# Products of the identity with itself on TensorE, in the openings and the router's end of a two-layer decoder

## The reference

```
x = x + attn0(ln(x)); x = x + xattn0(ctx, ctx, ln(x)); x = x + depths(ln(x))
x = x + attn1(ln(x)); x = x + xattn1(ln(x), ctx, ctx, mask); x = x + experts(ln(x))
```

## Time and profile before

| | |
|---|---|
| median of three runs | 2678.63 us (2676.26 to 2680.16) |
| profiled execution, its own time | 2679.13 us |
| its span | 2677.0 us |
| TensorE busy | 2317.4 us (87%) |
| VectorE, ScalarE, GpSimd busy | 1441.4, 1135.1, 738.9 us |
| mean granted clock of TensorE | 0.927 |

### The profile page before, as it was taken

One profiled execution on the slowest core, in us unless ns is written; L12 is line 12 of the kernel. 1 busy time (PEld: TensorE's weight loads), 2 busy tenths in 40 slices (PEclk: granted clock), 3 DMA queues, 4 the chain that ended last, 5 costly groups with the idle time before them and its releaser, 6 DMA issues. The chain is left out here.

```text
span 2677.0 us, 44222 instructions
## 1 busy us (share of the span) xinstructions
PE 2317.4 (87%) x13938; PEld 1441.6 (54%) x13939; DVE 1441.4 (54%) x3865; ACT 1135.1 (42%) x2659; POOL 738.9 (28%) x852
## 2 busy tenths in 40 slices
PE   4999999779984587679999999878888689999998
PEld 2455555445552344323444343344556489999997
DVE  3676666337764324267777777444554833343333
ACT  1666566423331324237777777522222023333332
POOL 3111111143322202323223222043331323333333
PEclk8999999889996799869999999978997799999999
DMA  4232222100001440022222222000005512222221
GB/s 149 73 96 92 77 85 85 37 3 5 5 1 57 66 71 1 18 84 72 67 66 72 72 65 71 23 27 9 9 5 210 183 32 34 36 37 35 35 34 25
DMA packets 134894, 148.75 MB, mean 56 GB/s; under 512 B 25374, under 2 KB 119240, under 8 KB 134600
## 3 DMA queue, kind: packets, MB, share of 16 engines
q1 hardware_dynamic: 121048, 128.83, 16.2%
q0 software_dynamic: 13680, 17.84, 4.1%
HBM read 100.71 MB, written 46.01 MB: 55 GB/s over the span
## 5 line engine op out<-in xcount | busy, mean ns | idle before, releaser
L447 ACT ACTIVATE self_probs<-self_score_ps 128x512 f32<-128x512 f32 (+3 forms) x1024 | 481.5, 516 | 331.9 <-PE self_score_ps L768 169.2
L586 DVE TENSOR_REDUCE self_neg_max<-self_max_ps 128x1 f32<-128x512 f32 x512 | 329.3, 686 | 157.3 <-PE self_max_ps L754 151.5
L754 PE MATMUL self_max_ps<-self_k_stack,self_q_stack 96*128 96x512 bf16 (+3 forms) x1024 | 355.4, 351 | 38.1 <-DVE self_neg_max L583 17.4
L765 PE MATMUL self_score_ps<-self_q_stack,self_k_stack 99*128 99x512 bf16 (+3 forms) x1024 | 345.1, 345 | 1.6 <-ACT self_probs L447 1.6
L2171 ACT ACTIVATE x_stream<-experts_up_ps,experts_bias_now 128x128 f32<-128x128 f32 x568 | 162.5, 369 | 373.2 <-PE experts_up_ps L2392 373.2
L583 DVE CUSTOM_DVE_ANT_0 self_masked<-self_max_ps,self_later 128x128 f32<-128x128 f32 (+3 forms) x512 | 235.3, 488 | 119.1 <-PE self_max_ps L754 107.7
L2392 PEld LDWEIGHTS experts_up_ps<-experts_tileT,x_stream 128*128 128x128 f32 x2272 | 266.7, 193 | 5.1 <-issue 1.6
L2392 PE MATMUL experts_up_ps<-experts_tileT,x_stream 128*128 128x128 f32 x2272 | 267.2, 276 | 1.2 <-DVE x_stream L2308 1.2
L2402 PE MATMUL experts_down_ps<-experts_down,x_stream 128*128 x1136 | 256.8, 379 | 0.0
L779 PE MATMUL self_out_ps<-self_probs,self_values 128*32 128x512 f32 (+3 forms) x2048 | 232.1, 525 | 3.3 <-ACT self_probs L447 1.4
L2402 PEld LDWEIGHTS experts_down_ps<-experts_down,x_stream 128*128 128x128 f32 x1136 | 210.4, 190 | 25.7
(11 more groups left out here) (281 smaller groups left out, 3804.8 us busy)
## 6 DMA issues: line engine op xcount, KB each, us to landing
self_parts_dram<-self_parts SPq DMA_DIRECT2D x64, 384.0 KB, 2.4
self_q_stack<-self_parts_dram SPq DMA_DIRECT2D x384, 64.0 KB, 2.3
self_k_stack<-self_parts_dram SPq DMA_DIRECT2D x384, 64.0 KB, 2.3
experts_up<-moe_up_dram SPq DMA_DIRECT2D x8, 1024.0 KB, 8.3
experts_down<-moe_down_dram SPq DMA_DIRECT2D x8, 1024.0 KB, 10.6
x_stream<-x_dram SPq DMA_DIRECT2D x8, 512.0 KB, 8.4
expert_rows_dram<-experts_down SPq DMA_DIRECT2D x8, 512.0 KB, 6.1
out_dram<-x_stream SPq DMA_DIRECT2D x8, 512.0 KB, 8.1
```

The lines of the kernel that those rows point to most:

```text
L447: act.activation(probs[:, i % 8, 0:w], score_ps[:, (16 * n + i) % 3, 0:w], ACT.Exp).then_inc(exp_done, 1)
L586: dve.tensor_reduce(neg_max[:, n % 2, t, h:h + 1], max_ps[:, i % 2, 0:w], AX, ALU.max, negate=True).then_inc(max_read, 1)
L754: last = pe.matmul(max_ps[:, i % 2, 0:w], q_stack[0:ROWS, h, P * t:P * t + P], k_stack[0:ROWS, h, 0:w], start=True, stop=True)
L765: last = pe.matmul(score_ps[:, m % 3, 0:w], k_stack[0:KROWS, head, P * j:P * j + P], q_stack[0:KROWS, head, S - w:S], start=True, stop=not ...
```

## The change

A helper, `spin`, issues a number of products of the identity with itself into a PSUM bank that nobody reads at that point. No semaphore is touched. It is called

- in both self-attentions: 24 products before TensorE's first waits; 4 before each sum of squares of the opening (with norms only); 12 (without norms) or 16 (with) behind the opening's part up to the maxima's turn; one behind each of the 32 first maximum tiles; 4 between the first sixteen and the turn of the maxima,
- in both cross-attentions: 20 before the first transposes, 4 before the first maxima, 6 before the third, 8 before the transposes of batch 2,
- in the routed one also 8, 8, 16 and 16 before the last two batches' `sr` and `bk`,
- in the depths stage: 60 before `attend(0)`.

```diff
@@ -52,6 +52,12 @@
         eng.sem_inc(passed)
     elif value > 0:
         eng.wait_ge(sem, value)
+
+
+def spin(pe, c, where, count):
+
+    for _ in range(count):
+        pe.matmul(where[:, 0:P], c.ident[:], c.ident[:], start=True, stop=True, skip_group_check=True)
 
 
 def make_constants(nc, c):
@@ -780,18 +786,25 @@
                                          start=(j == 0), stop=(j == TT - 1), tile_position=(0, 32 * h))
                     last.then_inc(pv_done, 1)
 
+                spin(pe, c, out_ps, 24)
                 pe.wait_ge(loaded, 16 * LOADS)
                 pe.wait_ge(scaled, 1)
                 pe.wait_ge(ready, 4 if causal else 3)
                 start_of_mt = opening.index(("mt", 0))
                 for use in opening[:start_of_mt]:
+                    if use[0] == "s":
+                        spin(pe, c, out_ps, 4)
                     side_work(*use)
+                spin(pe, c, out_ps, 16 if norm else 12)
                 for i in range(16):
                     max_tile(0, i)
+                    spin(pe, c, out_ps, 1)
+                spin(pe, c, out_ps, 4)
                 for use in opening[start_of_mt:]:
                     side_work(*use)
                 for i in range(16):
                     max_tile(1, i)
+                    spin(pe, c, out_ps, 1)
                 for n in range(N):
                     b, g = n // NG, n % NG
                     for j in range(TT):
@@ -1438,7 +1451,14 @@
                 WORK = {"xt": turn, "k": keys, "q": queries, "v": value_rows, "ot": turn_out, "ob": turn_back, "e": output,
                         "sr": spread_scores, "bk": turn_pick, "ch": gather, "S": scores, "M": maxima, "PV": with_values}
 
+                idle = {("xt", 0, 0): (out_ps[:, 0], 20), ("M", 0, 0): (out_ps[:, 0], 4), ("M", 0, 2): (out_ps[:, 0], 6),
+                        ("xt", 2, 0): (out_ps[:, 0], 8)}
+                if routed:
+                    idle.update({("sr", B - 2, 0): (max_ps[:, 0], 8), ("bk", B - 2, 0): (max_ps[:, 0], 8), ("sr", B - 1, 0): (max_ps[:, 0], 16),
+                                 ("bk", B - 1, 0): (max_ps[:, 0], 16)})
                 for step in steps:
+                    if step in idle:
+                        spin(pe, c, *idle[step])
                     m = place.get(step, 0)
                     if m >= 2:
                         pe.wait_ge(*bank_read(*uses[m - 2]))
@@ -1907,6 +1927,7 @@
                 pe.wait_ge(scaled, 1)
                 project(0)
                 pe.wait_ge(rest_loaded, 16 * (3 + FT))
+                spin(pe, c, out_ps[:, 0], 60)
                 attend(0)
                 project(1)
                 feed_forward(0)
```

## The result

The changed kernel takes 2654.43 us in the median of four runs (2651.66 to 2658.77); the kernel before took 2677.45 in the four beside them (2674.92 to 2680.16). The ratio is 0.9915, with a 95% interval of 0.9897 to 0.9933: 23.0 us faster, where 17.6 were forecast. The forecast time was 2661.5 in a range of 2652 to 2674; 2654.43 lies near its fast end. The profiled execution took 2655.91 us.

A forecast was written before the change was run, and what follows sets the result against it. The prediction blamed TensorE's lower clock after standing (390.7 of 2677 us), which unbroken products would lift. Gains 4.7 + 4 + 2.5 + 6.4 = 17.6 us off 2679.13 gave 2661.5, range 2652 to 2674 (8 in 10).

The forecast's parts named there:

- First self-attention, forecast 4.7: Opening of the first self-attention: +3.0 us up to the scores, +1.7 us from scores then running at full clock.
- the placing of the shifts: First self-attention: SyncE's three transfers, the last landing about 66.8, limit the gain before the scores to +3.0 us.
- unmoved by TensorE: First self-attention: SyncE would still issue its three shift transfers from 62.70 on.
- Cross-attentions' openings, 2.1 each: Both cross-attentions' openings: transposes, keys and queries gain, products before the third maxima cost 1.3; +4 us for both.
- the gap of 2 us at the barrier: Cross-attention start: if 20 products keep the clock up, transposes and keys win 3.2 us; at 6 in 10, +1.9.
- the gap between the first maxima: Cross-attention opening, 2.1 us without products: whether transposes and queries of batch 1 run full; half of 3.1, +1.5 us.
- Router's end, 2.5: Last two batches: last pick's turn and gather at full clock +2.0 us, the pick of the batch before +0.5.
- Depths, 0: Depths stage: 60 products end 13 us early in a 26.8 us wait, so scores start low as before: 0.
- Second self-attention, 6.4: Its opening: tiles +1.4 and +0.8, projection +2.3, scores +3.4, turned maxima +0.1, products before squares -1.6 us.
- Nothing moves: Rival: VectorE, GpSimd and SyncE set the openings and product cost eats the rest; within 5 us; chance 0.12.
- slower: Rival: products don't lift the clock and cost time where TensorE spins; 36 us, 2715 (18 if half); chance 0.08.
- The leaking hold: Rival: clock still falls in gaps without products, tiles with products run low for a while; 2666 to 2674; chance 0.18.

The follow-up runs named there:

- with_experts: Changed kernel without products before sums of squares and first and third cross-attention maxima, plus 20 before the expert stage's first transposes and 3 behind batches' logits: 2653.34 us.
- lean_third: `lean` plus 38 (first cross-attention) and 48 (second) products before the third transposes, and 22 instead of 16 before the last pick: 2646.53 us, ratio 0.9891.
- cross_only: Changed kernel with only the products in the two cross-attentions' openings kept: 2666.04 us, ratio 0.9957 against the kernel before.
- after_again: The changed kernel once more, unchanged, for a second profile: 2657.73 us, ratio 0.9927 against the kernel before.
- filled: Changed kernel without products before sums of squares and first and third cross-attention maxima, each other run made as long as its wait: 2642.38 us, ratio 0.9872.
- lean: Changed kernel keeping only products before the second transposes' maxima, behind tiles, 20 before cross-attentions' first transposes, 16 before the last pick: 2653.46 us, ratio 0.9906.
- self_only: Changed kernel with only the products of the two self-attentions kept: 2667.14 us, ratio 0.9961 against the kernel before.
- router_only: Changed kernel with only the products of the router's last two batches and the depths stage's 60 kept: 2671.78 us, ratio 0.998 against the kernel before.
- no_tiles: Changed kernel without the single product behind each maximum tile of both self-attentions: 2662.05 us, ratio 0.9942 against the kernel before.
- transposed: Changed kernel with each product replaced by two transposes of the identity: 2659.98 us, ratio 0.993 against the kernel before.

## Why the prediction was right, and where its sizes were off

**The bound and the mechanism** were right: lower clock behind standing of TensorE; unbroken products lift it (twelve behind the second transposes, from 39.40 on, with the clock up at 43.4); the projections, tiles, transposes and keys behind them ran at full rate, one by one as listed. In the profile of before TensorE is busy for 0.85 or more of the last 3.4 us ahead of each of the 33 rises of the clock, and for 0.65 or less ahead of each of the 33 falls; in that of after it is 0.93 or more and 0.57 or less, 27 of each. Busy isn't enough by itself: in `with_experts`, where the router's matmuls of 8 columns come between the products, TensorE shows busy for all 20.50 us from 2030.4 on, and the clock stays at 0.50. 0.23 us for a product at full clock holds (40 records in 4.70 us); no run of products is low throughout, but 6.33 us for the same 40 with 3.4 us of lower clock among them fits 0.47. The working from the earlier trace rows gives 18 records low and not 19, which changes nothing.

**First self-attention, forecast 4.7: 4.7 and 2.2 in the two profiles.** The tiles ran at full clock, the projection gave 2.3, and what is late next is the placing of the shifts:

```profile
60.84 3.98 SPq L263 DMA_DIRECT2D self_k_stack<-self_parts_dram  x6
64.86 1.97 SPq L271 DMA_DIRECT2D self_q_stack<-self_shift  x3
```

(SyncE in order of time, after.) Here one phrase of the prediction did not come true, that SyncE's issues stay where they were ("unmoved by TensorE"): they stand behind the stack loads in SyncE's queue and start at 64.86, 2.2 later than before. Two runs of six loads took 3.40 and 3.98 us instead of 2.77, which is 1.8 of it; what held them isn't shown. `lean_third` has the second of the two at 2.77 and its shifts at 63.43. In the changed kernel the first scores come at 68.01, behind a wait of 0.78 for them, and 1.8 are won where 3.0 were taken. The scores themselves then gave 1.6 (1.7 forecast). The rest of the 4.7 is 1.3 in the closing (its last projection 5.38 us, 6.70 before), which has 3.4 us of lower clock less in the first profile; in the second it has not, and the 2.2 are all from the opening. So 3.4 of the 4.7 are the products' work at most, and that the sum came out exact is luck.

**Cross-attentions' openings, 2.1 each: 4.1 and 3.5.** This is the one term that was mis-sized by its own working. It weighed the twenty products at 6 in 10, for the gap of 2 us at the barrier, and the queries of batch 1 at one half, for the gap between the first maxima. The clock held across the second gap in nineteen of the twenty openings that have the twenty products. It fell at the barrier in five of them (`cross_only`, `after_again`, `lean_third` and `filled` in the first cross-attention, `lean` in the second), and then the opening is 1.4 us longer, where the prediction took away the whole 3.2. The 3.5 of the second stage is in part no gain of the products: its opening takes 48.9 in `self_only` and `router_only`, which have none in it, and against that they win 2.0. The cost of the 4 and 6 products, 1.3, was right (1.4).

**Router's end, 2.5: 2.1**, 2.0 to 2.3 in the kernels that have the same products. That the clock would rise within the sixteen before the last pick was not shown by a row of before; after, they took 5.29 us, and the pick's turn and the gather behind them ran full, 0.64 and 1.89 us. **Depths, 0: 1.4 slower**, within what its profiles vary (240.8 to 245.2 with all sorts of edits).

**Second self-attention, 6.4: 6.1, for a wrong reason in part.** The steps are all there: tiles 0.60 apart, projection 3.70, squares later by 1.5. But kernels without a product in it (`cross_only`, `router_only`) have 628.6 too. Of the 5.9 us between these and before, 2.6 are the closing, low in before and not in them. The other 3.3 are in the opening: the first maximum tile, which waits for the keys' transfer, comes 1.0 to 1.1 us later in before, and from the first scores to the first product with the values it takes 7.8 us, in `router_only` 5.8, where the clock is up again 84 us into the stage instead of 90, and 4.7 after. So 2.0 of the 3.4 us that the sum took for those scores come without a product too. Against the 86.1 of `cross_only` and `router_only` the products win 2.6 in the opening, and 4.4 without those before the squares. That 6.1 is so near 6.4 is luck.

**Middle of the first cross-attention, not forecast: 3.6.** Its only products are the 8 before its last instruction, and `router_only`, which has those, has 244.7 as before. What differs is the number of single stretches such as 616.80 to 620.20 above (TensorE busy for all 3.40 us of it): three before, two after; and the stretch at its start, 17.1 us before, is 10.2. They fall elsewhere in many kernels of the table, though `cross_only` and the three profiles of kernels with the same products in that opening (after, `after_again`, `no_tiles`) all have 241.0 to 241.2; `transposed`, with as many, has 244.4. How far the opening's products decide where they fall is open. This and the openings (3.6 and 3.4 more than forecast), less the 1.4 of the depths stage, are the 5.4 us between 17.6 and 23.0, to within 0.3.

**The rivals.** Nothing moves and slower are out. The leaking hold is out as it was told, for in the changed kernel the gaps that it named kept the clock; what did leak there is the gap at the barrier, once in four openings (`after_again`, first cross-attention), and that is worth 1.4 us. The clock of this kernel falls anew before the openings of its stages, and the change doesn't take all that lies in that: `filled` wins 1.3% (35.7 of 2678) and has 176 us of lower clock left.

**Still open:** how much of `filled`'s further 9.5 us belongs to which products, what decides whether a closing or a barrier's gap falls to the lower clock, and why the first keys of the second self-attention land a microsecond later in before; two profiles of one kernel differ by up to 2.9 us in a stage, so single stages of that size aren't settled by one profile.

## What to carry to other kernels

Where TensorE's clock falls behind waits, as it did here (390.7 us of lower clock before, 176.4 in `filled`), idle time can be turned into speed by work that nobody reads, if it ends when the wait does: fill the wait to its end, and put single products into the short regular gaps of a consumer-paced loop, for these held the clock here (`no_tiles` was 4.3 us slower) while with the long runs before the loop alone it fell (at 1145.3). Don't put them between two instructions that already stand end to end (1.4 us lost in each cross-attention's opening, 1.9 in the second self-attention's), nor where another engine or a transfer sets the end (60 products in the depths stage: nothing). Before giving a stage's gain to the edit in it, look at the same stage in a kernel that is changed elsewhere, and at the lower clock inside it, which here went with most of what differed in a stage without an edit.

## What was not expected of the hardware

- The clock's level in a stage depends on what ran before and on when: a kernel changed only in the router's end and the depths stage had its second self-attention 5.9 us shorter, 2.6 of them in a closing that ran at full clock (last projection 3.69 us against 5.58). The same closing had 6.8 us of lower clock in after and none in `after_again`, the same program.
- Transposes of the identity lift the clock as matmuls do: 32 records in 4.91 us against 4.85, full clock behind both.
- The clock fell in the midst of evenly paced tiles (`no_tiles`, from 1145.3) and stayed full with one product behind each.
- The expert stage's opening spends 71.7 us at the lower clock with TensorE busy 46.3 of them, its DMA share at 1.01; broken up by products, the opening didn't get shorter.
